# Preparation of the conditioning vectors placed inside layer 0 of the first batch

## What is computed

```python
# layer 0 (H = 16 heads of 32), linear attention
xn = layernorm(x) * norm_scale + norm_bias
q, k, v = xn @ Wq + bq, xn @ Wk + bk, xn @ Wv + bv      # masked rows: k = -inf, v = 0
q, k = softmax(q, over the head's 32), softmax(k, over the 512 rows)
y = q @ (k.T @ v), head by head
scale, shift = split(silu(cond) @ film_emb_W + film_emb_b)          # 1024 x 1024
x1 = x + silu(layernorm_film(y) * (1 + scale) + shift) @ film_out_W + film_out_b
# layer 1
shift, scale, gate = split(silu(cond) @ W_ada + b_ada)              # 1024 x 1536
xm = layernorm_ln1(x1) * (1 + scale) + shift
attn = softmax attention of 8 heads of 64 on xm;  ssm = a state-space scan on xm
out = x1 + gate * silu(layernorm(concat(ssm, attn)) @ W_full + b_full)
```

## Time and profile before

| | us |
|---|---|
| median of 3 runs | 3960.05 (3959.69 to 3961.09) |
| the profiled execution, its own time | 3962.71 |
| span of that execution in the profile | 3960.8 |
| end of `setup`, first instruction of `attend` | 75.2 |
| first matmul of layer 1, batch 0 | 183.4 |
| first matmul of `mix` | 1538.2 |

### The profile page before, as it was taken

How to read it: one execution, slowest core, us unless ns; L and a number is a source line. 1 busy time by engine, 2 the same in 40 slices (tenths; PEclk the granted TensorE clock), 3 DMA queues, 4 the chain that set the end, 5 groups by cost and what they waited for, 6 DMA issues and landing times.

```text
span 3960.8 us, 36362 instructions
## 1 busy us (share of the span) xinstructions
PE 3387.0 (86%) x12362; PEld 1788.0 (45%) x12362; DVE 2718.3 (69%) x3459; ACT 2029.8 (51%) x3486; POOL 1893.9 (48%) x1139
## 2 busy tenths in 40 slices
PE   4899999999999998769888878888888888888758
PEld 1444444444444433444544544544544444544443
DVE  1344435344443533699898898997997997998992
ACT  1234343343433433846755755755765766676542
POOL 0021222212122211867667767766767766766661
PEclk8999999999999999668898898898898898888859
DMA  5001010100101010112122131222132122221111
GB/s 204 35 1 46 1 45 1 46 28 18 46 1 45 1 75 31 46 32 78 64 91 83 58 111 59 85 96 72 61 99 70 65 95 72 66 92 61 41 61 43
DMA packets 100937, 230.04 MB, mean 58 GB/s; under 512 B 10305, under 2 KB 10417, under 8 KB 97682
## 3 DMA queue, kind: packets, MB, share of 16 engines
q1 hardware_dynamic: 97186, 220.50, 16.5%
q10 hardware_dynamic: 3568, 7.21, 0.5%
HBM read 193.85 MB, written 33.83 MB: 57 GB/s over the span
## 4 chain that ended last, share of the span: by engine, by line
PE 18%; POOL 14%; DVE 14%; issue 13%; ACT 3%; DMA 0%; POOLq 0%; SPq 0%; DVEq 0%; ACTq 0%
POOL HS L1144 10%; PE bank L1505 10%; DVE HS L1383 6%; DVE acc L1388 5%; PE bank L1581 4%; PE bank L1522 3%; PE bank L1579 1%; DVE U L1420 1%; POOL delta L1159 1%; POOL ZS L1150 1%; ACT bank L1221 1%; POOL DU L1162 1%; POOL comb L1175 1%; PE bank L1531 0%; DVE G L1408 0%
## 5 line engine op out<-in xcount | busy, mean ns | idle before, releaser
L1144 POOL TENSOR_TENSOR HS<-DU,brep 128x1024 f32<-128x1024 f32 x512 | 1196.6, 2354 | 635.8 <-PE bank L1522 635.8
L1383 DVE TENSOR_TENSOR_SCAN HS<-bank,HS 128x1024 f32<-128x1024 f32 x512 | 1169.2, 2284 | 70.6 <-ACT bank L1221 58.0
L1522 PE MATMUL bank<-ident,HS 128*128 128x128 f32 x4096 | 686.8, 319 | 340.4 <-DVE acc L1388 305.4
L1221 ACT ACTIVATE bank<-delta,aneg 128x511 f32<-128x511 f32 x1024 | 662.0, 680 | 500.7 <-DVE HS L1383 498.6
L1522 PEld LDWEIGHTS bank<-ident,HS 128*128 128x128 f32 x4096 | 558.4, 164 | 616.3 <-DVE HS L1383 399.9
L446 POOL TENSOR_TENSOR PR<-PR,rrec 128x512 f32<-128x512 f32 x256 | 260.0, 1039 | 1128.6 <-DVE rrec L691 1128.6
L1388 DVE SCALAR_TENSOR_TENSOR acc<-bank,C,acc 128x512 f32<-128x512 f32 x960 | 668.4, 740 | 134.0 <-PE bank L1522 132.4
L1505 PE MATMUL bank<-XM,w_l 128*128 128x512 f32 x1024 | 499.8, 636 | 43.9 <-DVE U L1420 19.1
L1505 PE MATMUL bank<-w_l,G 128*128 128x512 f32 x1024 | 474.4, 609 | 7.3 <-ACT delta L1231 3.9
L523 ACT ACTIVATE PR<-bank,nsmax 128x512 f32<-128x512 f32 x256 | 173.5, 682 | 374.4 <-DVE nsmax L687 374.4
L757 PE MATMUL bank<-w_l,NT 128*128 128x512 f32 x768 | 342.6, 595 | 5.1 <-ACT NT L477 5.1
(11 more groups left out here) (169 smaller groups left out, 3877.8 us busy)
## 6 DMA issues: line engine op xcount, KB each, us to landing
brep<-b_d SPq DMA_DIRECT2D x256, 256.0 KB, 3.2
w_l<-in_L_cond_W_in SPq DMA_DIRECT2D x14, 2048.0 KB, 9.7
w_l<-in_L_cond_W_full SPq DMA_DIRECT2D x8, 2048.0 KB, 8.6
w_l<-in_L_cond_W_out SPq DMA_DIRECT2D x7, 2048.0 KB, 9.0
X<-in_x SPq DMA_DIRECT2D x8, 1024.0 KB, 5.2
x_d<-X SPq DMA_DIRECT2D x8, 1024.0 KB, 4.6
xm_d<-XM SPq DMA_DIRECT2D x8, 1024.0 KB, 3.9
ot_d<-OT SPq DMA_DIRECT2D x8, 1024.0 KB, 5.8
```

What stands on the lines that cost most here:

```text
L1144: nc.gpsimd.tensor_tensor(HS[:, u % DEEP], DU[:, chunks(j, s), :], brep[:, m % 3, :].unsqueeze(1).to_broadcast([P, UC, T]), ALU.mult).then ...
L1221: last = nc.scalar.activation(dA[:, s, i, 1:T], delta[:, c, 1:T], ACT.Exp, scale=aneg[:, c, n:n + 1])
L1383: nc.vector.tensor_tensor_scan(h, dA[:, u % 2].rearrange("p i t -> p (i t)"), h, 0.0, ALU.mult, ALU.add).then_inc(scanned, 1)
L1522: last = nc.tensor.transpose(y_bank[t % 2][:, i * P:(i + 1) * P], h, ident[:])
```

## The change

`setup` is gone, and its work stands in `attend`, within layer 0 of batch 0. SP's order is now x, the vectors, the mask rows, the mask, the weights Wk, Wq and Wv, and then the conditioning weights as five pieces of 1024 x 512 (2 MB each), with the film output weights between the second and the third. The pieces lie in memory that layer 1 uses later: both halves of `PR`, `QK`, and two thirds of the place of Wqkv; the fifth takes the room of the first once that has been multiplied, and Wqkv is loaded after the fourth. Bias rows, condition and other small tiles lie in `OT`, `V2` and `PT`. Two tables for TensorE and two for DVE give the slots of the five products and of the two sets of coefficients. The copy `cur` is gone: ACT reads `per_batch`. The waits for Wk, Wq, Wv and the film output weights stand at their first use. Everything after batch 0's layer 0, and all of `mix`, are as before.

```diff
+        room = [PR[:, 0].rearrange("p e t k -> p (e t k)"), PR[:, 1].rearrange("p e t k -> p (e t k)"), QK.rearrange("p i c t -> p (i c t)"),
+                wqkv.rearrange("p c n -> p (c n)")[:, 0:EC * D]]
+        piece = [room[j % 4].rearrange("p (c n) -> p c n", n=D) for j in range(5)]
...
+        row_bank, turn_bank = bank[6:8], (bank[5], bank[4])
+        PE_PIECE, PE_ROWS = (14, 15, 19, 20, 21), (18, 26)
+        DVE_PIECE, DVE_ROWS = (15, 16, 20, 21, 22), (19, 27)
...
             for g in range(SLOTS):
-                l0(n, g)
+                l0(0, g)
+                if conditioning:
+                    conditioning(g)
...
             def _(sp):
+                sp.dma_start(X[:], a["x"][0].rearrange("(t p) d -> p t d", p=P)).then_inc(x_in, 16)
+                for name, first, n in VECTORS:
...
+                sp.dma_start(maskrows[:], a["mask_BxS_ik0"].rearrange("b (t p) -> (b t) p", p=P)).then_inc(rows_in, 16)
                 load_mask(0)
+                for name in ("L0_cond_Wk", "L0_cond_Wq", "L0_cond_Wv"):
+                    load(sp, name).then_inc(arrived[name], 16)
+                load_piece(0)
+                load_piece(1)
+                load(sp, "L0_cond_film_out_W").then_inc(arrived["L0_cond_film_out_W"], 16)
+                load_piece(2)
+                load_piece(3)
+                sp.wait_ge(cond_mm, 1)
+                load_piece(4)
+                sp.wait_ge(cond_mm, 4)
+                load(sp, "L1_cond_Wqkv").then_inc(arrived["L1_cond_Wqkv"], 16)
+                sp.wait_ge(rows_done, 5)
+                sp.dma_start(gate_d, rows[4]).then_inc(gate_out, 16)
                 l0(0)
...
             def _(pool):
+                nc.gpsimd.memset(zeros, 0.0).then_inc(zeroed, 1)
...
                 def l0(n):
-                    if n:
-                        pool.wait_ge(*r0.done(n - 1, "x1", DC - 1))
-                    nc.gpsimd.tensor_copy(cur[:], per_batch[:, n, :]).then_inc(cur_done, 1)
...
             def _(act):
...
+                act.dma_start(cond, a["cond_2048"]).then_inc(cond_in, 16)
...
+                act.wait_ge(cond_in, 16)
+                nc.scalar.activation(scond, cond, ACT.Silu).then_inc(cond_silu, 1)
...
                     if g == ACT_TY:
+                        act.wait_ge(film_done, 1)
...
                         if c == 0:
                             act.wait_ge(xm_out, n * 16)
+                            act.wait_ge(ln1_done, 1)
...
             def _(dve):
+                def conditioning(g):
+                    for j in at(DVE_PIECE, g):
+                        dve.wait_ge(row_bias_in, 32)
+                        dve.wait_ge(cond_mm, j + 1)
+                        nc.vector.tensor_tensor(rows[j], row_bank[j % 2][0:B, :], rows[j], ALU.add).then_inc(rows_done, 1)
+                    for i in at(DVE_ROWS, g):
...
+                        dve.wait_ge(rows_turned, i + 1)
...
+                dve.wait_ge(rows_in, 16)
+                nc.vector.tensor_scalar(validrows[0:B * TT, :], maskrows[:], 1.0, None, ALU.not_equal).then_inc(valid_done, 1)
+                for t in range(TT):
+                    x_stats(0, t)
+                dve.wait_ge(turned_in, 1)
+                link(nc.vector.tensor_copy(cols[:], bank[3][:, 0:NCOL]))
...
+                inv_std_end(0, 0)
...
                 dve.wait_ge(bias_in, 3 * 16)
                 dve.wait_ge(blocks_done, P // DH0)
-                for t in range(TT):
-                    x_stats(0, t)
-                inv_std_end(0, 0)
-                l0_alone(l0, 0)
+                l0_alone(l0, conditioning)
...
             def _(pe):
+                def conditioning(g):
+                    for j in at(PE_PIECE, g):
+                        if j == 0:
+                            pe.wait_ge(condT_done, 1)
+                        pe.wait_ge(piece_in[j], 16)
+                        if j >= 2:
+                            pe.wait_ge(rows_done, j - 1)
+                        for c in range(EC):
+                            last = nc.tensor.matmul(row_bank[j % 2][0:B, :], condT[:, c, :], piece[j][:, c, :], start=(c == 0), stop=(c == EC - 1))
+                        last.then_inc(cond_mm, 1)
+                    for i in at(PE_ROWS, g):
+                        pe.wait_ge(rows_done, 2 * i + 2)
+                        for k in range(2 * DC):
+                            src = (film, ada)[i][:, k * P:(k + 1) * P]
+                            last = nc.tensor.transpose(turn_bank[i][:, k * B:(k + 1) * B], src, ident[0:B, 0:B])
+                        last.then_inc(rows_turned, 1)
```

More of the change, by code:

```diff
@@ L154, in build @@
             X = sb("X", [P, TT, D], c=early)
[L155 to L156 removed]
+            attend(nc, a, bank, ident, cols, col, bq8, aneg, convw, per_batch, gate_d, x1_d, xm_d, ot_d, X, W, load, load_wide, arrived)
         mix(nc, a, out, space, bank, ident, col, aneg, convw, x1_d, xm_d, ot_d, gate_d, b_d, wide, load_wide, arrived)
[L160 to L254, removed]
[L255 to L294 removed]
@@ L297, in attend @@
[L297 removed]
+def attend(nc, a, bank, ident, cols, col, bq8, aneg, convw, per_batch, gate_d, x1_d, xm_d, ot_d, X, W, load, load_wide, arrived):
     ctx = ExitStack()
@@ L330, in attend @@
         veps, spare, nmr = sb("veps", [P, TT]), sb("spare", [P, 1]), sb("nmr0", [P, TT])
+        room = [PR[:, 0].rearrange("p e t k -> p (e t k)"), PR[:, 1].rearrange("p e t k -> p (e t k)"), QK.rearrange("p i c t -> p (i c t)"),
+                wqkv.rearrange("p c n -> p (c n)")[:, 0:EC * D]]
+        piece = [room[j % 4].rearrange("p (c n) -> p c n", n=D) for j in range(5)]
+        film, ada = OT.rearrange("p c t -> p (c t)")[0:B, 0:2 * D], V2.rearrange("p t d -> p (t d)")[0:B, 0:3 * D]
+        rows = [film[:, 0:D], film[:, D:2 * D]] + [ada[:, k * D:(k + 1) * D] for k in range(3)]
+        cond, scond = (PT.rearrange("p k e t -> p (k e t)")[0:B, k * E:(k + 1) * E] for k in range(2))
+        spot = OT.rearrange("p c t -> p (c t)")
+        vecrows, validrows, zeros, condT, scale1 = (spot[:, 2 * D + k * P:2 * D + (k + 1) * P] for k in range(5))
+        condT, scale1 = condT[:, 0:EC * B].rearrange("p (c b) -> p c b", b=B), scale1[:, 0:2 * DC * B].rearrange("p (i c b) -> p i c b", i=2, b=B)
+        maskrows = sb("maskrows", [B * TT, P], I32)
         bias_in = sem("bias_in")
@@ L509, in l0 @@
                             act.wait_ge(xm_out, n * 16)
-                        from_ring(XM[:, c, :], ACT.Identity, n, "x1", c, scale=cur[:, LN1_A + c:LN1_A + c + 1], bias=cur[:, LN1_B + c:LN1_B + c + 1])
+                            act.wait_ge(ln1_done, 1)
+                        from_ring(XM[:, c, :], ACT.Identity, n, "x1", c, scale=per_batch[:, n, LN1_A + c:LN1_A + c + 1],
+                                  bias=per_batch[:, n, LN1_B + c:LN1_B + c + 1])
                 def l1(b, n):
@@ L735, in l1 @@
                                 l0(n, 1 + hp * 2 * TT + h)
+                link = Link(dve, own_set, 7)
+                link.begin(0)
+                def conditioning(g):
[4 more added lines that the diff above has]
+                    for i in at(DVE_ROWS, g):
+                        sc, sh, at_a, at_b, gain, shift, done = (
+                            (0, 1, FILM_A, FILM_B, "L0_cond_film_norm_scale", "L0_cond_film_norm_bias", film_done),
+                            (1, 0, LN1_A, LN1_B, "L1_cond_ln1_g", "L1_cond_ln1_b", ln1_done))[i]
+                        dve.wait_ge(rows_turned, i + 1)
+                        y = turn_bank[i][:, 0:2 * DC * B].rearrange("p (k c b) -> p k c b", k=2, b=B)
+                        link(nc.vector.tensor_scalar(scale1[:, i], y[:, sc], 1.0, None, ALU.add))
+                        for first, v in ((at_a, gain), (at_b, shift)):
+                            for c in range(DC):
+                                last = nc.vector.tensor_scalar(per_batch[:, :, first + c], scale1[:, i, c, :], col(v, c), None, ALU.mult)
+                        link(last)
+                        dst = per_batch[:, :, at_b:at_b + DC].rearrange("p b c -> p c b")
+                        link(nc.vector.tensor_tensor(dst, dst, y[:, sh], ALU.add))
+                        nc.vector.memset(spare[:], 0.0).then_inc(done, 1)
```

105 lines of the change are left out of this document (54 added, 51 removed).

## The result

The changed kernel takes 3923.51 us (median of 4 runs, 3922.48 to 3924.82) against 3959.87 of the kernel before (3957.59 to 3961.09): ratio 0.9907, 95% interval 0.9892 to 0.9923. It is faster by 36.4 us, where 60.1 were forecast; 3923.5 lies 12.5 us above the top of the range. The profiled execution took 3922.48, with a span of 3920.7.

What follows compares the result with a forecast made beforehand. TensorE was taken to bound the kernel up to layer 1's start in batch 0. Terms -70.8 + 6.9 + 2.9 + 0.9 = -60.1 us took the profiled 3962.71 us to 3902.6, median 3900.0; range 3893 to 3911.

Steps and rivals of the forecast that it cites:

- Rival B: At the start, transfers bind: mask rows land at 12.4 us, clock rises late; 3905.5 us, or 3909; chance 0.2.
- Step 2: Two film products (pieces 0, 1) in layer 0's V slots: 16 matmuls, nothing hides them, 6.9 us lost.
- Step 3, the three products after Y: Around the first layer norm: 24 matmuls, 10.3 us, fill the idle 7.41 us; film output 2.9 us later.
- Step 1: Setup leaves the path: statistics of x start at 9.7 us instead of 80.83, K near 22.0; 70.8 us gained.
- The clock at the start: K after the transposes of x at the new start: full speed expected, nothing charged; upper bound 2.6 us.
- My counter case: Setup's first film product took 9.5 us for 16 matmuls, 6.9 at 0.43 us each: a 2.6 us loss.
- Step 3, the silu table: Transposes of normalised Y: table already in place, so the first tile reaches ACT 0.7 us after they start.
- Step 4: Ada set at the film output: eight transposes (0.66 us) and 0.25 us of DVE work left over; 0.9 us lost.
- a move of this distance: Layer 1's first product to the end, 3777.4 us: moving by over 2 us would make the whole forecast wrong.
- the allowance of 2 us: Last stage: could react to the shift, so 2 us added either way, no more.
- Rival C: Products all on the path: TensorE's idle time stays, 11.0 us lost in place of 2.9; 3908 us; chance 0.07.
- if nothing of the 10.3 us were hidden: Three products around the first layer norm, none hidden: film output later by 10.3 + 0.7 = 11.0 us.

Runs made afterwards that it cites:

- e1: Changed kernel with half of the contraction left out in the two film products (pieces 0 and 1), for timing only: 3919.51 us, ratio 0.9890.
- e2: Changed kernel with half of the contraction left out in the three ada products (pieces 2 to 4), for timing only: 3915.73 us, ratio 0.9880.
- e9: Changed kernel with half of the contraction left out in all five conditioning products, for timing only: 3908.14 us, ratio 0.9864.
- e4: Changed kernel with conv weights loaded later on SP, mask rows issued ahead of x, statistics of x ahead of validrows: 3923.02 us, ratio 0.9899.
- e6: Changed kernel with the silu table loaded right after the normalisation of Y in batch 0, instead of at first use: 3920.90 us, ratio 0.9895.
- e0: The changed kernel run again without edits, beside the kernel before: 3926.68 us, ratio 0.9912.
- e10: Changed kernel with the gate's product moved from slot 21 to 28 (addition to 29) and the silu table loaded early: 3909.97 us, ratio 0.9869.

## Why the prediction was wrong

The mechanism was right, sign included: none of the five products waits for a transfer, they fill the idle time of the layer norm as forecast, and the rest of the kernel moves forward with layer 1's first product. The step that failed is the size of the moved work: the terms of steps 2 and 3 take a product as 8 matmuls of 0.43 us, 3.4 us, and it is 16, 6.9 us. Both of Rival B's events came, too, the late landing and the late clock, with 4.0 us together. Two small terms missed besides. In the profiled execution, layer 1 starts at 147.55 where the forecast had 123.3. The 24.2 us are, term by term:

* **Step 2, the two products in the V slots, +7.0.** "16 matmuls" are 32; 62.53 to 69.50 and 73.12 to 80.09 are 13.9 us, not 6.9. e1 shows it: half of the work gives back 6.9.
* **Step 3, the three products after Y, +10.5.** "24 matmuls, 10.3 us" are 48 and 20.7 (94.65 to 115.35). Y to transposes takes 25.2 us (90.13 to 115.35) instead of 14.8. e2 and e9 show it.
* **Step 1, the start, +2.3.** I chose 9.5 us for the mask rows, nearer to the lower bound, because little traffic was ahead of them; they landed at 12.23, at the upper bound. The choice was wrong, the bounds held. e4 shows small transfers and x holding each other: put first, the mask rows land at 2.7 (issued at 0.75, 1.9 us to landing), and then x (10.8 for 9.55) and the vectors (13.7 for 12.1) land later.
* **The clock at the start, +1.7.** I charged nothing, because the same sequence had run fast at 88 to 93 us. In the eleven profiled executions of the changed kernel and its variants in which K follows the first transposes of x, it ran fast in four (13.97 us for 32 products) and slow in seven (15.71 to 16.30). My counter case, the setup's first product with its 2.6 us, was the better guide.
* **Step 3, the silu table, +1.2.** The forecast had 3.7 us from the transposes (157.6) to the film output (161.3), and they are 4.87. "Now the table is in place" was wrong: its load waited for the tile, as row 116.09 shows, and e6, with 3.59, gives its 1.28 us back.
* **Step 4, the film output, +1.4.** 0.9 was forecast and 2.3 measured (27.33 us from the film output to layer 1, against 24.99 before); in e6, where the film output is fast, they are 25.77, so the ada set costs 0.8, near the forecast, and the half-speed start of the film output 1.6. It goes with the item before: e6 removes both.

That is 24.1 of 24.2. From there on the execution won 4.2: layer 1's first 24 products were fast in this one (-2.0), the attention stage behind them 0.7 longer, and the last stage 2.9 shorter (2419.7 against 2422.6 us). This is luck: in e0, the same program, the last stage is 2423.2 and the whole distance 3776.6, and e0 comes out at 3926.6. Without it the forecast would have missed by 24 us, not 20 (3902.6 and 3922.5 for the profiled execution). The forecast had named a move of this distance (3777.4) by more than 2 us as a sign that it was wrong as a whole. It moved by 4.2 here and by 0.8 in e0, and by 7.0 in e10, so the allowance of 2 us was too small to tell chance from an effect of the change.

Rival B had the landing and the clock about as they came (2.9 and 2.6 us, measured 2.3 and 1.7), 3905.5, but with the same product count it could not reach the result. Rival C ("the idle time stays") did not happen: TensorE has no gap after Y. The bound "if nothing of the 10.3 us were hidden" was thought to be the worst case of step 3. It bounded what could be hidden and took the amount of work as known, and so the range, built on it, ended at 3911. Three numbers ahead of the result spoke against the count: the "16 matmuls" of the clock paragraph, the x32 of the film products, and the setup's 106 rows on TensorE, of which the five products are 80.

The rule that the Trainium skill states, "TensorE: Matmul & The Clock Gate", section Part 4: PE-mode transpose, was set aside in the prediction on one instance. By it K would begin at half speed, and in seven of eleven executions it did. In the other four only transposes of different kinds had run, and K was fast from the first, as in the kernel before. So these runs show neither the rule nor its opposite as a law.

## What to carry to other kernels

Count the work of a moved step in the trace, by the rows of its line and its first and last start, and not by the calls in the code; an fp32 product here is two rows for each call, a transpose one. The check is cheap: the step's own stretch (here 32.5 to 69.5 us for five products, 7.4 each and 6.9 at full speed) has to come out of count times duration. And when a piece of work is put where TensorE has no idle time, look for the consumer's date first: the gate's product was needed by nobody in this stage, and one entry in each of two slot tables put it into an idle gap, for 7.2 us and a faster start of what follows.

## What the runs showed of the hardware that was not expected

* A gap of TensorE can cost more than its length. With the second layer norm's gap left open, the 24 products behind it took 12.2 to 12.6 us in seven of eight executions; filled, 10.54 in six of six. At the silu table, with 2.7 us of idle time in a 4.9 us stretch, the clock was 0.58 behind it; with 1.35 us it stayed at 1.00. It is not so behind every gap: in the kernel before, TensorE was idle for 7.41 us ahead of the transposes of the normalised Y; these took 3.27 us where they take 2.24 without a gap (e6), but the film output behind them ran at full speed (14.00 us for 32).
* PEclk reads 1.00 from the start of the execution, also where products run at half speed: in the kernel after it is 1.00 from 24 to 28 us, and TensorE has 5 products there against 10 or 11 in the stretches behind. At the very start the spacing of the rows tells the clock, and that column does not. The kernel after:

```profile
24.00:28.00 4.00, 3.69 (x5) 1.00 1.04 387
28.00:32.00 4.00, 4.00 (x10) 1.00 1.04 387
```

* In the kernel after, the silu table's load stands behind two waits of ACT in the code (the film coefficients, then the first transposed tile) and starts only when the tile is there, at 116.09. In the kernel before there was one wait, and the load started right behind the layer norm, ahead of the tile, and was over when ACT took it at 155.31, 1.26 us after the transposes had begun. e6 shows that the load need not wait for the tile; that the second wait is what held it was not tested by a run of its own. The kernel before, ACT:

```profile
154.02 1.28 ACT L477 ACT_TABLE_LOAD   x1
```
